# Routing lists built in two parts, twelve token tiles ahead of the last projection and four behind the router, and two moves in TensorE's order

## The reference

```
x = x + retention(layernorm(x), ctx, ctx)              # 16 heads of 16
x = x + fp8_linear(layernorm(x))                       # 256 -> 256
x = x + cross_attention(layernorm(x), ctx) @ Wproj.T + b
x = x + moe(layernorm(x)):
    logits = x @ router.T + bias                       # 8 experts
    w = softmax(top 4 of logits), scattered to (N, 8)
    out_e = down_e( (up + 1) * gate * sigmoid(1.702 gate) ), hidden 512, clipped at 7
    y = sum over e of w_e * out_e
```

## Time and profile before

| | us |
|---|---|
| median of three executions | 985.96 |
| the profiled execution's own time | 991.85 |
| its span, first to last instruction | 990.1 |
| TensorE busy in the span | 808.7 (82%) |
| VectorE busy | 634.9 (64%) |
| ScalarE busy | 493.2 (50%) |
| GpSimd busy | 286.3 (29%) |
| `phase_a` ends, `phase_m` begins | 617.8 |

### The profile page before, as it was taken

The page is one execution under the profiler, slowest core; times in us unless marked ns, Lnnn a source line. Parts: engine busy times, 40 slices in busy tenths (PEclk is TensorE's granted clock), DMA queues, the critical chain, the costliest instruction groups (busy, mean ns, idle before and its releaser), DMA issues. The chain is left out here.

```text
span 990.1 us, 18525 instructions
## 1 busy us (share of the span) xinstructions
PE 808.7 (82%) x6324; PEld 508.7 (51%) x6324; DVE 634.9 (64%) x1238; ACT 493.2 (50%) x950; POOL 286.3 (29%) x261
## 2 busy tenths in 40 slices
PE   0682776778876888987887798899999999999993
PEld 0341332233432434432242225489899989998993
DVE  4546657787678876886779932845666666665652
ACT  1210310454353553436548572157777777777772
POOL 6005002210040100001001000236666666666643
PEclk9796688759997997987867799789999999999997
DMA  8421362014230161102544311314444444444432
GB/s 279 115 67 57 110 182 79 32 44 129 49 113 33 37 194 34 49 23 96 178 144 139 120 64 43 109 34 66 67 67 66 66 67 67 66 67 66 65 47 32
DMA packets 72072, 83.22 MB, mean 84 GB/s; under 512 B 10288, under 2 KB 65200, under 8 KB 71856
## 3 DMA queue, kind: packets, MB, share of 16 engines
q1 hardware_dynamic: 57008, 61.25, 20.3%
q0 software_dynamic: 14976, 20.78, 13.0%
HBM read 52.71 MB, written 29.29 MB: 83 GB/s over the span
## 5 line engine op out<-in xcount | busy, mean ns | idle before, releaser
L1600 PE MATMUL gu_ps<-xt,w 128*128 128x256 f16 x1872 | 219.6, 275 | 1.2 <-ACT xt L1321 1.2
L672 ACT ACTIVATE p<-st 128x512 f32<-128x512 f32 x256 | 139.1, 597 | 137.9 <-PE st L1156 137.1
L883 DVE TENSOR_REDUCE neg_max<-sc 128x2 f32<-128x1024 f32 x128 | 156.5, 1222 | 61.9 <-PE sc L1132 60.6
L1600 PEld LDWEIGHTS gu_ps<-xt,w 128*128 (+1 forms) x1872 | 182.6, 99 | 23.6 <-issue 1.9
L1391 POOL DMA_INDIRECT out<-y,block_rows x78 | 125.4, 1608 | 103.4 <-ACT y L1351 83.0
L1614 PE MATMUL dn_ps<-w,h 128*128 (+1 forms) x936 | 108.6, 273 | 0.3 <-DVE h L1518 0.3
L1383 POOL DMA_INDIRECT gx<-xr_d,block_rows x78 | 86.0, 1102 | 51.5 <-DVE block_rows L1491 28.6
L1132 PE MATMUL sc<-kz,sq 48*128 48x512 f16 x256 | 61.9, 453 | 45.9 <-DVE neg_max L883 41.4
L1614 PEld LDWEIGHTS dn_ps<-w,h 128*128 128x128 f16 x936 | 91.5, 98 | 11.2 <-issue 0.6
L580 POOL COPY rden_rows<-rden 128x512 f32<-128x512 f32 x16 | 10.7, 668 | 282.3 <-DVE rden L904 250.1
L1509 DVE TENSOR_SCALAR up<-up 128x512 f32<-128x512 f32 x78 | 33.4, 428 | 83.0 <-ACT up L1337 82.9
(11 more groups left out here) (200 smaller groups left out, 1108.6 us busy)
## 6 DMA issues: line engine op xcount, KB each, us to landing
stack_d<-t SPq DMA_DIRECT2D x16, 256.0 KB, 2.4
raw<-in_gate_up_t SPq DMA_DIRECT2D x4, 1024.0 KB, 5.2
raw_next<-in_gate_up_t SPq DMA_DIRECT2D x4, 1024.0 KB, 5.5
sq<-stack_d SPq DMA_DIRECT2D x16, 192.0 KB, 3.6
kz<-stack_d SPq DMA_DIRECT2D x16, 192.0 KB, 4.7
sq<-stack_d SPq DMA_DIRECT2D x32, 96.0 KB, 2.4
kz<-stack_d SPq DMA_DIRECT2D x32, 96.0 KB, 2.3
ctx_pad<-in_ctx SPq DMA_DIRECT2D x4, 512.0 KB, 4.3
```

What stands on the lines that cost most here:

```text
L672: act.activation(p32[:, n // 2 % RING, 2 * (n % 2) + i, :], st[:, i, :], ACT.Exp, scale=QSCALE).then_inc(s_exp, 1)
L883: dve.tensor_reduce(neg_max[:, qt, :, pair], sc[:], AX.X, ALU.max, negate=True).then_inc(m_max, 1)
L1600: ins = pe.matmul(gu_ps[:, 2 * half + g, q * ROWS:(q + 1) * ROWS], weights(i, wi, slice(col, col + P)), xt[:, i % 2, kd, xi, :], start=(j ...
```

## The change

In `phase_a`, new steps build the lists of the first 12 tiles (`FIRST`) in the last batch: `list_load` (SyncE) brings one table of numbers (884 KB, float16) into `raw` in place of two loads of 512 KB at the start of `phase_m`; `list_pre` (TensorE, 13 matmuls) counts; `list_place`, `list_high` and `list_low` (VectorE, 6, 2 and 8 instructions) make places and one-hots; `list_rows` (TensorE, 12 matmuls for each of the 8 experts) makes the lists; `list_take` copies them. The places of the new `ORDER` lines set where each stands among the old steps. In `phase_m` only the last 4 tiles are listed, with 4 matmuls for each expert and one-hots of 512 elements, and added to the first part. A token that was not chosen gets a negative place, so the counts are not needed first. The spare matmuls before the last `den`, `den_turn` and `o_proj` go, `turn4` has 20, `lists` 16 instead of 20, `look_up` 4 instead of 8, `turn_x` 2 instead of 4. The lists of experts 2 to 7 stand between `gate_up(0, 0)` and `gate_up(0, 1)`; before, 2 and 3 stood ahead of both and 4 to 7 behind both. VectorE's `unit(0)` moves behind the taking of all lists. For block 37 `down` moves ahead of `gate_up(38, 1)`. `chosen` becomes float16.

```diff
+LIST_NO = (("low_no", (P, FIRST)), ("high_no", (HI, E * FIRST)), ("lower", (P,)), ("ones", (P,)), ("token", (E * FIRST,)),
+           ("token_last", (E * T,)))
...
+def list_parts(raw, raw_next):
...
+    parts["high_token"] = room(HI * E * FIRST // 2).bitcast(F16).rearrange("p (h x) -> p h x", h=HI)
+    parts["rows_first"] = room(E * HI)
...
+    parts["low_hot"] = raw_next[:].bitcast(F16).rearrange("p (n l t) -> p n l t", l=P, t=FIRST)
...
+            def list_load(b, _):
+                sp.wait_ge(w_lo, (E - 1) * WP)
+                sp.dma_start(lists["numbers"], t["list_no"]).then_inc(list_in, 16)
...
+            def list_place(b, _):
+                done, _ = counted(list_step, 0)
+                pre = sc[:, 1, 0:E * (FIRST + 1)].rearrange("p (e t) -> p e t", e=E)
+                dve.wait_ge(list_pre, 1)
+                done(dve.tensor_copy(base[:], pre[:, :, FIRST]))
+                done(dve.scalar_tensor_tensor(lists["unchosen"], chosen[:, :, 0:FIRST], -1.0,
+                                              route_const["behind"][:, None, 0:FIRST].to_broadcast([P, E, FIRST]), ALU.add, ALU.mult))
+                done(dve.scalar_tensor_tensor(lists["place"], pre[:, :, 0:FIRST], -MIDDLE, lists["unchosen"], ALU.add, ALU.add))
+                done(dve.tensor_scalar(lists["high"], lists["place"], 1 / P, ROUND, ALU.mult, ALU.add))
+                done(dve.tensor_scalar(lists["high16"], lists["high"], ROUND, None, ALU.subtract))
+                done(dve.scalar_tensor_tensor(lists["low16"], lists["high16"], -float(P), lists["place"], ALU.mult, ALU.add))
+
+            def list_high(b, _):
+                done, _ = counted(list_step, 6)
+                over = lambda a: a[:, None, :].to_broadcast([P, HI, E * FIRST])
+                dve.wait_ge(list_in, 16)
+                done(dve.tensor_tensor(lists["high_token"], lists["high_no"], over(lists["high16"].rearrange("p e t -> p (e t)")), ALU.is_equal))
+                done(dve.tensor_tensor(lists["high_token"], lists["high_token"], over(lists["token"]), ALU.mult))
+
+            def list_low_(b, e):
+                need(dve, list_mm, e - LOW_HOT + 1)
+                dve.tensor_tensor(lists["low_hot"][:, e % LOW_HOT], lists["low_no"],
+                                  lists["low16"][:, e, None, :].to_broadcast([P, P, FIRST]), ALU.is_equal).then_inc(list_low, 1)
+
+            def list_take(b, _):
+                dve.wait_ge(list_mm, E)
+                dve.tensor_copy(lists["rows_first"], sc[:, 1, 256:256 + E * HI]).then_inc(list_took, 1)
...
             def den(b, q):
-                stay_awake(AWAKE["den"])
+                if (b, q) != (LAST, QUADS - 1):
+                    stay_awake(AWAKE["den"])
...
             def den_turn_(b, q):
-                stay_awake(AWAKE["den_turn"])
+                if (b, q) != (LAST, QUADS - 1):
+                    stay_awake(AWAKE["den_turn"])
...
             def o_proj(b, u):
...
-                if u == 0:
-                    stay_awake(AWAKE["o_proj"])
...
+            def list_pre_(b, _):
+                pe.wait_ge(m_cp, B * QUADS)
+                pe.wait_ge(list_in, 16)
+                pe.wait_ge(choose_step, LAST * CHOOSE_STEPS)
+                pre = sc[:, 1, 0:E * (FIRST + 1)].rearrange("p (e t) -> p e t", e=E)
+                pe.matmul(pre, lists["lower"], chosen[:, :, 0:FIRST + 1], start=True, stop=False, skip_group_check=True)
+                for i in range(FIRST):
+                    ins = pe.matmul(pre[:, :, i + 1:], lists["ones"], chosen[:, :, i:i + 1].to_broadcast([P, E, FIRST - i]),
+                                    start=False, stop=(i == FIRST - 1), skip_group_check=True)
+                ins.then_inc(list_pre, 1)
+
+            def list_rows(b, e):
+                pe.wait_ge(list_low, e + 1)
+                for i in range(FIRST):
+                    ins = pe.matmul(sc[:, 1, 256 + e * HI:256 + (e + 1) * HI], lists["low_hot"][:, e % LOW_HOT, :, i],
+                                    lists["high_token"][:, :, e * FIRST + i], start=(i == 0), stop=(i == FIRST - 1))
+                ins.then_inc(list_mm, 1)
...
-            sp.dma_start(high_no, t["high_no"]).then_inc(no_in, 16)
-            sp.dma_start(low_no, t["low_no"]).then_inc(no_in, 16)
-            sp.wait_ge(rt, CHOOSE_STEPS + WEIGH_STEPS)
+            sp.wait_ge(rt, PLACE_STEPS + WEIGH_STEPS)
...
             choose_experts(dve, done, logit[:, LAST, :], const["before"], tmp, chosen[:, :, LAST])
-            assert count[0] == CHOOSE_STEPS
-            dve.wait_ge(sums_mm, 1)
-            dve.tensor_copy(tile_sums[:], tr_ps[:, 0, 0:1].to_broadcast([P, P])).then_inc(sums_ok, 1)
+            done(dve.scalar_tensor_tensor(unchosen[:], chosen[:, :, LAST], -1.0, const["behind"][:, None, LAST].to_broadcast([P, E, T]),
+                                          ALU.add, ALU.mult))
+            done(dve.scalar_tensor_tensor(unchosen[:], unchosen[:], -MIDDLE, base[:, :, None].to_broadcast([P, E, T]), ALU.add, ALU.add))
+            assert count[0] == CHOOSE_STEPS + 2
+            dve.wait_ge(pre_mm, 1)
+            done(dve.tensor_tensor(place[:], pre[:, :, 0:T], unchosen[:], ALU.add))
+            done(dve.tensor_scalar(high[:], place[:], 1 / P, ROUND, ALU.mult, ALU.add))
+            done(dve.tensor_scalar(high16[:], high[:], ROUND, None, ALU.subtract))
+            done(dve.scalar_tensor_tensor(low16[:], high16[:], -float(P), place[:], ALU.mult, ALU.add))
+            assert count[0] == PLACE_STEPS
             dve.wait_ge(rt_exp, 1)
             weigh_experts(dve, done, tmp, chosen[:, :, LAST], combine[:, LAST, :])
-            assert count[0] == CHOOSE_STEPS + WEIGH_STEPS
-
-
-            dve.wait_ge(pre_mm, 1)
-            pre = tr_ps[:, 1, 0:P].rearrange("p (e t) -> p e t", e=E)
-            dve.tensor_copy(token16[:], per_tile(const["token"]))
-            done(dve.tensor_copy(counts[:], tr_ps[:, 1, P:P + E]))
-            done(dve.scalar_tensor_tensor(after[:], pre, -1.0, per_expert(counts), ALU.mult, ALU.add))
-            done(dve.tensor_tensor(after[:], after[:], per_tile(const["token"]), ALU.add))
-            done(dve.tensor_tensor(gap[:], pre, after[:], ALU.subtract))
-            done(dve.tensor_tensor(gap[:], gap[:], chosen[:], ALU.mult))
-            done(dve.tensor_tensor(place[:], after[:], gap[:], ALU.add))
-            done(dve.tensor_scalar(high[:], flat(place), 1 / P, 0.5 / P - 0.5, ALU.mult, ALU.add))
-            done(dve.tensor_scalar(high[:], high[:], ROUND, None, ALU.add))
-            done(dve.tensor_scalar(flat(high16), high[:], ROUND, None, ALU.subtract))
-            done(dve.scalar_tensor_tensor(flat(low16), flat(high16), -float(P), flat(place), ALU.mult, ALU.add))
-            dve.wait_ge(no_in, 2 * 16)
-            done(dve.tensor_tensor(high_hot[:], high_no[:], flat(high16)[:, None, :].to_broadcast([P, HI, P]), ALU.is_equal))
-            done(dve.tensor_tensor(high_token[:], high_hot[:], flat(token16)[:, None, :].to_broadcast([P, HI, P]), ALU.mult))
+            assert count[0] == PLACE_STEPS + WEIGH_STEPS
+            done(dve.tensor_tensor(high_hot[:], lists["high_no"][:, :, 0:E * T], over(flat(high16)), ALU.is_equal))
+            done(dve.tensor_tensor(high_token[:], high_hot[:], over(lists["token_last"]), ALU.mult))
 
             def low_one_hot(e):
-                need(dve, rows_mm, e - HOT + 1)
-                dve.tensor_tensor(low_hot[:, e % HOT], low_no[:], low16[:, e, None, :].to_broadcast([P, P, NT]),
+                dve.tensor_tensor(low_hot[:, e], lists["low_no"][:, :, 0:T], low16[:, e, None, :].to_broadcast([P, P, T]),
                                   ALU.is_equal).then_inc(low_ok, 1)
 
             def take_rows(g):
                 first, last = GROUPS[g]
+                at = slice(first * HI, last * HI)
                 dve.wait_ge(rows_mm, last)
-                dve.tensor_copy(rows[:, first * HI:last * HI], dn_ps[:, g % 2, first * HI:last * HI]).then_inc(rows_ok, 1)
+                dve.tensor_tensor(rows[:, at], dn_ps[:, g % 2, at], lists["rows_first"][:, at], ALU.add).then_inc(rows_ok, 1)
                 dve.wait_ge(rows_ok, g + 1)
 
             def lay_table():
 
-
+                done(dve.tensor_tensor(counts[:], pre[:, :, T], base[:], ALU.add))
...
             list_rows(1)
             for e in range(2, E):
                 low_one_hot(e)
-            unit(0)
-            low_half(0)
             take_rows(2)
             take_rows(3)
             for i in range(2, GX + 1):
                 list_rows(i)
+            unit(0)
+            low_half(0)
             unit(1)
             low_half(1)
             take_share(0)
...
                 pe.wait_ge(low_ok, e + 1)
                 g = next(g for g, (first, last) in enumerate(GROUPS) if first <= e < last)
                 need(pe, rows_ok, g - 1)
-                for tile in range(NT):
-                    ins = pe.matmul(dn_ps[:, g % 2, e * HI:(e + 1) * HI], low_hot[:, e % HOT, :, tile], high_token[:, :, e * NT + tile],
```

(45 more changed lines are left out.)

78 lines of the change are left out of this document (44 added, 34 removed).

## The result

The changed kernel took 984.15 us in the median of 20 executions (977.64 to 993.56), the kernel before 991.32 in the median of 20 beside them (984.24 to 995.27); the ratio is **0.9945, 95% interval 0.9921 to 0.997**. Two of the 20, 992.37 and 993.56, lie over 1.5% above the fastest and count as slow; the ratio of the means is 0.995 with them and 0.994 without.

A forecast was written before the change was run, and what follows sets the result against it. Bounds: the serial end of `phase_a`, VectorE then lists at the start of `phase_m`, and the tail. 0.85 + 0.25 + 1.65 + 1.4 - 11.6 + 1.8 = -5.65 against the median 985.96 gives 980.3 us, range 974.5 to 987.5.

The forecast's parts named there:

- the start of `phase_m`: From `chosen` to `gate_up(1, 1)`: shorter lists and an earlier first gather bring that step forward, -11.6 us.
- The clock in `phase_a`: Last `values` to `o_proj`: without wide spare matmuls TensorE's clock halves, rising 3 us into `o_proj`; +1.4 us, bounds 0 and +7.
- `list_pre`: End of `phase_a`: 13 small matmuls ahead of the score at place 1289 all count, +0.85 us.
- `den_turn`'s queue: End of `phase_a`: `list_rows(1)` and `(2)` replace six spare matmuls right ahead of `den_turn`, +0.25 us.
- The one-hot ahead of `o_add(1)`: End of `phase_a`: `list_low(7)` waits for `list_rows(3)` behind `o_proj(1)`, delaying the second `o_add`, +1.65 us.
- The tail: Last blocks: `collect(37)` stays behind `unit(77)`, which the moved `down(37)` delays; +1.8 us, bounds 0 and +2.6.
- within 1%: Whole kernel: a measurement tells about 1% (9.9 us) from no change; chance 0.83 of staying within.
- The first: `o_proj` and after: the clock is not given back in `o_proj`; 9.1 us more, 989.4 us, chance 0.1.
- The second: Start of `phase_m`: gain half lost, -8 instead of -11.6, up to 2 more in `phase_a`; 984 to 986, chance 0.25.
- The third: Whole kernel: tail and clock cost nothing and the front gives all; 976.2 us, chance 0.12.
- the fourth: `phase_a`: early lists don't stand where their places say, issued early by `banks_free`; time near The second's, chance 0.03.

The follow-up runs named there:

- e8: The changed kernel with each tile of the low one-hot contiguous instead of one element in twelve; 990.48 us in one execution.
- e1: The changed kernel with the last early one-hot and its list moved behind the second `o_add`; 982.85 us, ratio to the kernel before 0.9931.
- e11: e9 without most spare matmuls among the lists of experts 4 to 7 and before the last `route`; 974.77 us, ratio to the kernel before 0.9884.
- e4: The changed kernel with the spare matmuls before the last `den`, `den_turn` and `o_proj` back; 981.43 us, ratio to the kernel before 0.9931.
- e5: The changed kernel with early lists behind `o_proj` and the layer norm's sums, spares back as in e4, none of the 20 before `turn4`; 985.71 us.
- e7: The changed kernel with the edits of e5 and e6, eight spare matmuls behind `turn_x(1)` and the old order of `down`; 977.04 us, ratio 0.9873.
- e6: The changed kernel with 20 spare matmuls instead of 4 while the table is looked up; 982.88 us, ratio to the kernel before 0.9931.
- e9: e7 with one-hots of experts 4 to 6 waiting for GpSimd's last layer-norm steps, expert 7's one-hot and list later; ratio to the kernel before 0.9905.
- e10: The same kernel as e7, run once more beside e9; ratio to the kernel before 0.9891.
- e2: The changed kernel with TensorE's old order, `down(37)` behind `gate_up(38, 1)`; 984.55 us, ratio to the kernel before 0.9956.
- e3: The changed kernel, `down(37)` still moved, with `collect(37)` and `scale_y(37)` put ahead of `unit(77)`; 983.55 us, ratio to the kernel before 0.9965.

## Why the prediction failed, though its time came out

The step that failed is the start of `phase_m`, -11.6 for a measured -9.5, and within it `gate_up(1, 0)`, which I took at full clock (2.62 us) and which ran mostly at half (4.46). The clock in `phase_a` was the right mechanism at too small a size. The other terms held within 0.35 us.

- **`list_pre`: +0.85, measured +0.54.** I took 0.065 us a matmul from the earlier trace rows, whose weights lie 32 bytes apart (weight load 0.174). Those of `list_pre` are contiguous: 0.54 us for 12, and a load of 0.10. The other lists of `phase_m` (step of 8 bytes, load of 0.117) took 0.95 for 24, not 1.6. e8 shows the step as the cause.
- **`den_turn`'s queue: +0.25, measured +0.28.** From the start of the last `values`, `den_turn` came 4.32 after and 4.04 before.
- **The one-hot ahead of `o_add(1)`: +1.65, measured 1.50** in C. e1 shows that it was this wait, and that undoing it gives half, the rest of VectorE's work being in the chain too; in e11, where that work is out of the way as well, C is back at 8.97.
- **The clock in `phase_a`: +1.4, measured +2.05.** The mechanism is as predicted (fall at 595, rise at 602), and e4, e5 and e7 hold the clock by putting the spares back. The term was 0.65 short: 1.56 in `o_proj`, and `den_turn` at half clock, which I had not priced (1.09 for 0.60). The rule of the Trainium skill that I set against it (TensorE: Matmul & The Clock Gate, "HAM oscillation": the throttle comes with idle waits) would have given 0; the rows at 595 show a fall at busy 1.00. Where TensorE did wait (e6, `gate_up(1, 0)` behind 2.13 us), spares in the wait went with full clock in all four traces (e7, e9, e10, e11), as the rule has it; but e1 kept full clock behind a wait of 2.02 us without them.
- **Start of `phase_m`: -11.6, measured -9.5** (E). Up to `gate_up(1, 0)` the forecast held in its sum: it has `gate_up(0, 0)` 14.2 us after `chosen` starts and `gate_up(1, 0)` 24.8, and they came 14.16 and 25.12 after it. But that was in part luck, since errors cancel on the way. The store of the shares did not bind: it landed in 1.7 us, not 3.3 or 4.8, and the first gather went out 6.9 us after `chosen` starts (7.2 in the forecast), though the first rows came late: after 5.7 us, not 5.0, because the count stood behind spare matmuls at half clock. `gate_up(0, 0)` ran wholly at half clock (5.08 for my 3.9), the lists behind it took 0.95 for my 1.6. From the start of `gate_up(1, 0)` to that of `gate_up(1, 1)` it then took 4.74 us where I had 3.1, and this is most of what was missing. e1 is the check: with `gate_up(1, 0)` at full clock it took 3.08, and E was 28.15, against the 27.9 of the forecast. I had the half clock as a bound (-9.8), which is nearly what came. The one-hots of 512 elements at 0.4 and their place were right.
- **What I had let pass there.** With 4 spare matmuls left of 8, TensorE idled 4.47 us in the wait for the table, and its clock was at half from 633 to 643. By e6 this is worth 3.0 us.
- **The tail: +1.8, measured +1.8,** by the mechanism named; e2 gives 1.7 back, e3 shows that the move gains nothing in another order.
- **Sum.** By stretches: +0.5 (`list_pre`), +0.8 (A), +1.6 (B), +1.5 (C), 0 (D), -9.5 (E), +1.8: -3.3, which is the difference of the spans (-3.4) but for rounding. A ratio of 0.9945 is -5.4 us, and my sum was -5.65. This agreement is in part luck: 3.3 us would be a ratio of 0.9967, which the interval holds too (-3.0 to -7.8 us), and the scatter ahead of the last `values` is larger than the gap. Whether the change gains something there as well, one trace of the kernel before can't show. Nor did the absolute time come from the sum alone: the kernel before, 985.96 in my three executions, had a median of 991.32 in twenty.
- **Two readings in the prediction were off,** without weight. The row at 650 (0.57) puts the fall of the clock at 650.1, not 650.6. And 60 list matmuls and 20 spare ones are 8.8 us at the prices given, not 8.3; they took 8.1.
- **The chances.** The size was forecast right as a ratio, and still 0.83 went to "within 1%" on the ground that less can't be told. What a measurement tells depends on how many executions stand behind it, and three that lie 7 us apart say little of twenty.
- **Rivals.** The first (clock kept at half through `o_proj`) did not come: it rose after 3 us. The second, half of the front lost, is nearer to what happened than its chance of 0.25: E is -9.5, by the half clock it names. The third needed a free tail and a free clock, and neither was. Nor did the fourth come: in the trace the early lists stand where their places say.

## What to carry to other kernels

Small matmuls are no cover for the clock: work moved into TensorE's waits displaced the spare matmuls that had kept it, and the wide matmuls behind paid. Put each moved step where none of the chain stands behind it in any queue, and when VectorE fills a wait, look whether GpSimd is in the chain at that moment. When a stretch gets faster, fill the new waits too: here E went from 29.86 to 24.63, more than the 3.3 us of the change itself by stretches, though 1.7 of it is one `gate_up` that e1 had at full clock without filling. And look at how many executions will be compared before you call a small gain one that can't be told.
